# First dense layer of a graph network by groups of four destination tiles, with its sums kept turned

## The reference

```python
x = layernorm(x + attention_block(x, src, dst, etype))
h = x
for W_r, W_sl, W_el in [(W_r1, W_sl1, W_el1), (W_r2, W_sl2, W_el2)]:
    msg = (rel_embed[etype] + h[src]) @ W_r
    agg = segment_sum(msg, dst)
    self_msg = where(in_degree == 0, h @ W_el, h @ W_sl)
    h = rrelu(agg * deg ** -0.5 + self_msg)          # rrelu: slope 11/48 below 0
x = layernorm(x + h)
```

## Time and profile before

| | us |
|---|---|
| median of 3 runs | 2772.72 (2772.16 to 2774.16) |
| profiled execution | 2772.09 |
| its span in the trace | 2770.1 |
| POOL busy | 1590.8 (57%) |
| PE busy | 2148.2 (78%) |
| DVE busy | 2044.5 (74%) |
| ACT busy | 1222.7 (44%) |
| mean granted TensorE clock | 0.906 |

### The profile page before, as it was taken

One profiled execution on the slowest core, in us unless ns is written; L12 is line 12 of the kernel. 1 busy time (PEld: TensorE's weight loads), 2 busy tenths in 40 slices (PEclk: granted clock), 3 DMA queues, 4 the chain that ended last, 5 costly groups with the idle time before them and its releaser, 6 DMA issues.

```text
span 2770.1 us, 45483 instructions
## 1 busy us (share of the span) xinstructions
PE 2148.2 (78%) x16208; PEld 1803.9 (65%) x16208; DVE 2044.5 (74%) x4582; ACT 1222.7 (44%) x3215; POOL 1590.8 (57%) x1672
## 2 busy tenths in 40 slices
PE   1467666677677677787787788788787999999998
PEld 0355555566566566576676677667666876888887
DVE  6889998888888888898888888888887456333333
ACT  1265566555455555555555555555654323000000
POOL 6767777777777777777777777777774000000000
PEclk9888888888888888888889988999898999999999
DMA  8535554454554554554555555555444344666664
GB/s 222 164 117 166 174 172 141 149 176 146 157 181 145 157 182 150 154 184 152 166 176 157 169 175 164 172 169 174 154 153 153 108 157 135 215 209 212 215 211 158
DMA packets 184632, 463.50 MB, mean 167 GB/s; under 512 B 86336, under 2 KB 113784, under 8 KB 164577
## 3 DMA queue, kind: packets, MB, share of 16 engines
q1 hardware_dynamic: 116050, 339.10, 36.3%
q0 software_dynamic: 53600, 114.17, 15.8%
q10 hardware_dynamic: 14752, 7.26, 1.0%
HBM read 362.54 MB, written 97.84 MB: 166 GB/s over the span
## 4 chain that ended last, share of the span: by engine, by line
POOL 52%; PE 24%; issue 18%; DVE 4%; DMA 2%; ACT 0%; POOLq 0%; ACTq 0%; SPq 0%; DVEq 0%
POOL arena L568 52%; PE pair L960 19%; PE bank L884 1%; DVE arena L1124 1%; PE bank L845 1%; PE pair L933 1%; DMA wlp<-n_L_gnn_loop_weight_dram 1%; PE pair L963 1%; DMA group_starts<-endv 0%; DMA arena<-in_x_dram,srcw 0%; DVE arena L1101 0%; PE pair L814 0%; PE pair L791 0%; DVE arena L1071 0%; DVE arena L1072 0%
## 5 line engine op out<-in xcount | busy, mean ns | idle before, releaser
L568 POOL DMA_INDIRECT arena<-rows,srcw x1617 | 1540.4, 953 | 510.1 <-issue 492.2
L1124 DVE TENSOR_TENSOR arena<-bank,idx 128x2000 bf16<-128x2000 bf16 (+3 forms) x700 | 560.5, 853 | 22.4 <-PE pair L814 19.0
L960 PE MATMUL pair<-arena 125*125 125x384 bf16 x3285 | 551.4, 326 | 1.6 <-DVE arena L1325 1.6
L814 PE MATMUL pair<-arena 128*128 128x250 bf16 x2500 | 344.5, 285 | 262.2 <-DVE arena L1124 208.7
L590 ACT ACTIVATE arena<-pair 99x264 f32<-99x264 f32 (+2 forms) x410 | 278.8, 712 | 582.6 <-PE pair L814 448.9
L960 PEld LDWEIGHTS pair<-arena 125*125 125x125 bf16 x3285 | 447.4, 136 | 103.3 <-issue 8.4
L684 ACT ACTIVATE arena<-arena,wexp 128x128 f32<-128x128 bf16 x1650 | 487.4, 387 | 1.6
L884 PE MATMUL bank<-arena 128*125 128x130 f32 x3300 | 486.9, 319 | 0.0
L884 PEld LDWEIGHTS bank<-arena 128*125 128x125 f32 x3300 | 476.4, 230 | 3.9
L814 PEld LDWEIGHTS pair<-arena 128*128 128x128 bf16 x2500 | 237.8, 102 | 339.7 <-DVE arena L1124 271.5
L1101 DVE TENSOR_TENSOR arena<-arena,bank 128x4224 bf16<-128x4224 int16 x150 | 344.2, 2350 | 1.7
(11 more groups left out here) (250 smaller groups left out, 2311.5 us busy)
## 6 DMA issues: line engine op xcount, KB each, us to landing
arena<-counts SPq DMA_DIRECT2D x106, 812.5 KB, 4.4
counts<-arena SPq DMA_DIRECT2D x50, 1562.5 KB
arena<-dst SPq DMA_DIRECT2D x50, 1056.0 KB
arena<-etype SPq DMA_DIRECT2D x50, 1056.0 KB
arena<-rows,srcw POOLq DMA_INDIRECT x1617
arena<-counts SPq DMA_DIRECT2D x14, 281.2 KB, 2.7
edge_terms<-arena SPq DMA_DIRECT2D x200, 12.4 KB
xt<-in_x_dram SPq DMA_DIRECT2D x50, 62.5 KB
```

What stands on the lines that cost most here:

```text
L568: pool.indirect_dma_start(out=rows[:, q, c, :], out_offset=None, in_=rows0, in_offset=bass.IndirectOffsetOnAxis(ap=srcw[:, q, c:c + 1], ax ...
L814: r = pe.matmul(group_of(n, gi), ohl[:, sl, gi * GC + c, :], ohm[:, sl, gi * GC + c, :], start=(c == 0), stop=(c == GC - 1))
L960: r = pe.matmul(o, ring[0:TN, m % RD, h - h0, :], hs[k][0:TN, h, :], start=(h == first), stop=(h == last - 1))
L1124: return v.tensor_tensor(hot_.rearrange("p c (j t) -> p c j t", t=2), iotap[:, 0:w].rearrange("p (j t) -> p j t", t=2)[:, None, :, :].broa ...
```

## The change

The first layer's products are turned round: each 128-column part of `hs0` is a weight, and the counts of four destination tiles (500 columns) move. A **unit** is one source tile (or one half of the types) for a group of four destination tiles, and is three products of 500 columns into one bank, so that the three parts and all units add up there. The tiles make 13 groups (the last has two tiles) of 52 units. The sum stands turned (features on partitions), without the factor `norm`, in `acc`. That factor is put into layer 2's weights side instead (`scale=norm` in `node_a`), and the layer's own term is divided by it (`rstd`) and turned once (`own_turned`).

`row` and `early` go. In their place each tile t from 6 on has up to two **stretches** (t,0) and (t,1) of at most 12 units, all from counts loaded back in **chunks** of at most 4 units (512 KB, rows of 1000 B) into two buffers `held`. There are 80 stretches with 528 units in 154 chunks; 148 units are left behind the main loop, 40 of them for tiles 44 to 47 and 52 half-wide ones for tiles 48 and 49. 24 tiles have a third chunk in stretch (t,0): 9, 13, 17, 21, 22, 25, 26, 29, 30, 33, 34, 35, 37, 38, 39 and 41 to 49 (of 2, 3 and 1 units in tiles 9, 22 and 44, else of 4). The first chunk of (t,0) runs ahead of the sums (L884 before), the second and third behind the edge terms. Stretch (t,1) has up to 4 units until tile 30, 5 or 6 in tiles 31 to 40, 7 to 9 from tile 41 on.

The last tile's batches, which stood ahead of its `weights`, now stand behind them as in all tiles. `hot` shrinks to 26 slots, and some small tiles move into the arena.

```diff
 def sp_fast(sp):                      # the loop over t
+                load_held(t, 0, 1)
                 if t + 2 < NT:
                     load_wide(t + 2, f2)
-                if t in EARLY:
-                    load_early(t)
+                load_held(t, 0, 2)
                 if t + 1 < NT:
                     reshape_terms(t + 1)
                 else:
                     for m in range(RD):
                         load_piece(m)
+                load_held(t, 1, 0)
+                load_held(t, 1, 1)
                 if t < NT - 1:
                     store_x1(t)
+                load_held(t, 1, 2)
+                load_held(t + 1, 0, 0)
                 store_counts(t)
...
+            def load_held(t, k, i):
+                if (t, k, i) not in HELD_AT:
+                    return
+                n = HELD_AT[t, k, i]
+                key, g, u0, u1 = HELD[n]
+                if n >= 2:
+                    sp.wait_ge(s("held_done"), n - 1)
+                sp.wait_ge(s("at_stored"), 32 * GT * (g + 1))
+                sp.dma_start(held[:, n % 2, 0:GT * (u1 - u0) * TN].rearrange("p (t f) -> p t f", t=GT),
+                             counts[GT * g:GT * g + GT, :, u0 * TN:u1 * TN].rearrange("t p f -> p t f")).then_inc(s("held%d" % (n % 2)), 16)
...
 def pe_fast(pe):
+            def unit(o, moving, u, start, stop):
+                for j in range(3):
+                    js = slice(j * D, (j + 1) * D)
+                    if u < 2:
+                        n_ = (P, R2)[u]
+                        w = relW[0:n_, 0, u, js]
+                    else:
+                        n_ = TN
+                        w = hs0[0:TN, u - 2, js]
+                    r = pe.matmul(o, w, moving[0:n_], start=start and j == 0, stop=stop and j == 2)
+                return r
...
+            def stretch(t, k, i):
+                if (t, k, i) not in HELD_AT:
+                    return
...
+                if i == 0 and m >= 1:
+                    pe.wait_ge(s("st_read"), m)
+                if u1 > 2:
+                    pe.wait_ge(s("hs_ready"), u1 - 2)
+                pe.wait_ge(s("held%d" % (n % 2)), 16 * (n // 2 + 1))
...
             for t in range(NT):
...
+                stretch(t, 0, 0)
                 if t >= 1:
                     pe.wait_ge(s("fin"), t)
                 pe.wait_ge(s("wm"), NWM * t + 1)
...
                 if t + 1 < NT:
                     terms(t + 1)
-                if 1 <= t < NT - 1:
-                    row(t - 1)
+                stretch(t, 0, 1)
+                stretch(t, 0, 2)
...
+                    stretch(t, 1, 0)
+                    for j in range(4, BT):
                         batch(t, j)
-                    x1_in(t)
-                    batch(t, BT - 1)
-                    x1_node(t)
-                    if t in EARLY:
-                        early(t)
+                x1_in(t)
+                stretch(t, 1, 1)
+                x1_node(t)
+                stretch(t, 1, 2)
...
             for m in range(LOWER):                      # behind the main loop
+                k, g, u0, u1 = PIECES[m]
...
+                for u in range(u0, u1):
+                    if u == HS - 1 and g == 0:
+                        pe.wait_ge(s("hs_ready"), NT)
+                    r = unit(o, part[:, :, u - u0, :], u, u == DONE_U[g], u == HS - 1)
+                r.then_inc(s("piece_done"), 1)
...
+                if u1 == HS and g >= 1:
+                    for t in tiles_of(g - 1):
+                        node_m(t)
 def dve_fast(v, link):
             def weights(t):
+                if t >= 1:
+                    stretch_sum(t - 1, 1)
...
+            def stretch_sum(t, k):
+                v.wait_ge(s("held_done"), HELD_TO[t, k])
+                v.wait_ge(s("ev"), seq("node", GT * g + GT - 1) + 1)
+                a = acc[:, GT * g:GT * g + GT, 0:TN]
+                v.tensor_tensor(a, per_tile(bank[6][:, 0:GT * TN], GT), a, ALU.add).then_inc(s("st_read"), 1)
...
                     for j in range(2):
                         batch(t, j)
-                    prepare_edges(t + 1)
+                    if more:
+                        prepare_edges(t + 1)
+                    stretch_sum(t, 0)
                     batch(t, 2)
...
-                    batch(t, 4)
-                    row_sum(t - 1)
-                    for j in range(5, BT):
+                    for j in range(4, BT):
                         batch(t, j)
```

More of the change, by code:

```diff
@@ L75, with tiles_of @@
 L0_LINKS = 37
[L76 to L89, removed]
+GT = 4
+NGR = -(-NT // GT)
+HOTS = 26
+NU = 4
+SLEN = 3 * NU
+STRETCH, DONE_U = {}, [0] * NGR
+for t_ in range(6, NT):
+    for k_ in range(2):
+        best = None
+        for g_ in range(NGR - 1):
+            n_ = min(SLEN, t_ + 1 + k_ - DONE_U[g_])
+            if GT * g_ + GT + 1 <= t_ and n_ >= 2 and STRETCH.get((t_, 0), (NGR,))[0] != g_ and (best is None or n_ > best[0]):
+                best = (n_, g_)
+        if best is not None:
+            n_, g_ = best
+            STRETCH[t_, k_] = (g_, DONE_U[g_], DONE_U[g_] + n_)
+            DONE_U[g_] += n_
+STRETCHES = list(STRETCH)
+HELD, HELD_AT, HELD_TO = [], {}, {}
+for key_ in STRETCHES:
+    g_, u_, e_ = STRETCH[key_]
+    for i_ in range(-(-(e_ - u_) // NU)):
+        HELD_AT[key_ + (i_,)] = len(HELD)
+        HELD.append((key_, g_, u_ + i_ * NU, min(u_ + i_ * NU + NU, e_)))
+    HELD_TO[key_] = len(HELD)
+def tiles_of(g):
+    return range(GT * g, min(GT * g + GT, NT))
+PIECES, GROUP_TO = [], []
+for g_ in range(NGR):
+    each_ = RD_WORDS // (TN * len(tiles_of(g_)))
+    for u_ in range(DONE_U[g_], HS, each_):
+        PIECES.append((0, g_, u_, min(u_ + each_, HS)))
+    GROUP_TO.append(len(PIECES))
 LOWER = len(PIECES)
@@ L119 @@
             SEQ["turned", t_ + 1] = len(SEQ)
-    if t_ in EARLY:
-        SEQ["early", t_] = len(SEQ)
+    SEQ["node", t_] = len(SEQ)
 class Chain:
@@ L202, in build @@
         toh = carve([P, C, R], BF16)
+        HOTB_AT = at_[0]
         here(TOH_AT)
-        hot = carve([P, C, P])
-        HOTB_AT = at_[0]
+        hot = carve([P, HOTS, TN])
+        assert at_[0] <= HOTB_AT
+        here(HOTB_AT)
         hotb = carve([P, C, P], BF16)
@@ L676, in act_fast @@
                     node_b(0, t - 1)
-                if t == NT - 1:
-                    for j in range(BT):
-                        batch(t, j)
+                    own_turned(t - 1)
                 act.wait_ge(s("z_ready"), t + 1)
@@ L864, in pe_fast @@
                     self_in(t + 1)
-                else:
-                    row(t - 1)
-                    for j in range(BT):
-                        batch(t, j)
                 pe.wait_ge(s("th_ready"), t + 1)
@@ L883, in pe_fast @@
                         pe.wait_ge(s("wm"), NWM * t + c // WMG + 1)
-                    r = pe.matmul(sums[0:TN, 0:D + 2], hot[:, c, 0:TN], rows[:, q, c, 0:D + 2], start=(c == 0), stop=(c == C - 1))
+                    r = pe.matmul(sums[0:TN, 0:D + 2], hot[:, c % HOTS, :], rows[:, q, c, 0:D + 2], start=(c == 0), stop=(c == C - 1))
                     if c in ACC_AT:
```

351 lines of the change are left out of this document (159 added, 192 removed).

## The result

The changed kernel takes **2892.99 us** (median of 4 runs, 2886.86 to 2897.46) against 2773.22 of the kernel before: ratio 1.043, 95% interval 1.0418 to 1.0442. It is 120 us slower. The forecast was 2820, 48 slower, and its range ended at 2872: the direction was right, the size was not. The profiled execution has a span of 2893.2 us.

What follows compares the result with a forecast made beforehand. It took POOL's gathers (41.3 us a tile) to bound the main loop and PE the tail; 2772.1 - 48 (tail and last tiles) + 96 (lag from late third chunks) = 2820 us, slower, range 2735 to 2872.

Steps and rivals of the forecast that it cites:

- Tail: Behind the main loop: 61 + 17 + 12 x 3.75 + about 4 = 127 us, 51 us shorter than before.
- Last tiles: Batches now behind the last tile's sums: 42.5 us for tile 48, 40 for tile 49, ending 5 us later.
- The sum without a lag: Whole kernel with the main loop at POOL's pace: 51 + 2 - 5 = 48 us gained on 2772.1.
- Third chunk late: Main loop, stretch (t,0): the chunk lands at +29.9 behind the lists, PE idle from +20.0; lag adds up to 96 us.
- Rival (a): Third chunk isn't late, being served beside the lists; lag under 10 us, 2724 to 2734 us, faster; chance 0.13.
- What is behind the lists comes after them: SP's queue in the main loop: lists are through at +26.7, then the chunk's 512 KB lands at +28 to +30.7.
- I take 3.2: PE's time for the third chunk's products after idling, between 2.5 us at full clock and 5.1 at half.
- 3 us given back in each tile between: Main-loop tiles without a late third chunk have 2 to 5 us of room; each recovers 3 us of any lag.
- the wait for the gathers that I took as room: Main loop, tile 47: DVE waits 3.70 us for the gathers, read as some 3 to 4 us a tile free for work.
- the end of this lag: Main loop's upper case: chunk at +31, half clock, node product in full, 3 us more a tile, lag 150.

Runs made afterwards that it cites:

- a7: Changed kernel with the third chunk's load ahead of the lists and DVE's sum of (t-1,1) later, behind `u`: 2726.4 us.
- d12: Changed kernel with only the third chunk's load moved ahead of the lists: 2728.3 us, 0.9827 to 0.9860 of the kernel before.
- d14: Changed kernel with the third chunk's load issued from ACT's own DMA queue, not SP's: 2895.7 us, 1.0416 to 1.0464 of the kernel before.
- c10: Changed kernel with 88 unused products keeping PE busy between second and third chunk: 2862.9 us, 1.0309 to 1.0344 of the kernel before.
- b9: Changed kernel without the main loop's stretches (their loads, products and sums left out): 2711.4 us, 0.9770 to 0.9802 of the kernel before.

## Why the prediction was wrong in size

By its own steps:

- **Tail, right.** First tail product at 2335.99, first product of the second layer 2461.68: 125.7 us, forecast 127. From `u`(49) to the end: 599.2 us, forecast 40 + 127 + 434 = 601. The two 500-column sums of a group take 0.68 us each, forecast 0.66.
- **Last tiles, nearly.** `u`(48) to the first tail product: 85.4 us, forecast 82.5.
- **The sum without a lag, right.** 2772.1 - 48 = 2724. The kernels without the wait took 2726.4 and 2728.3 (a7, d12), and a7's `u`(49) is at 2121.8, where 2078.5 + 42.5 = 2121.0 was forecast.
- **Third chunk late, right, with its time.** Forecast +29.9; PE gets it at +28.4 to +31.1, +29.8 on average, in the 13 tiles from 33 on, and at +30.7 to +31.8 in the nine before them, where the edge terms end 1.7 us later too (+19.3). The idle time is 8.4 to 10.8 us, 9.5 on average, forecast 9.9. In tile 45 the chunk's packets move from +26.1 to +29.0. Rival (a) is out.
- **Its reason, half right.** "What is behind the lists comes after them" holds, but it isn't only the queue's order: with a queue of its own the chunk comes no earlier (d14).
- **"I take 3.2", wrong.** In nine of the 19 tiles with four units in the third chunk its products ran wholly at half the clock, as in tile 45: 5.16 us, 2.0 more. In the other ten they took 4.1 to 5.1. The prediction had 5.1 as its end and took the value between. DVE gets batch 2 at +36.0 on average, forecast +34.25, and the 22 tiles take 49.4 us: together 179.6 us over 41.25, where the steps have 134.6, that is 45 more, or 2.0 a tile. Of this c10 shows 30 as the clock's.
- **"3 us given back in each tile between", wrong.** The 17 tiles between tile 9 and 47 take 40.5 us and give back 13.2 us in all, where 38.6 were forecast: 25 more. The eleven up to tile 24 take 39.8 us on average and give back 1.5 each; the six from 27 on take 41.2 to 42.8 and give back nothing. b9 shows why for up to 1.9 us of each early one: the wait for the gathers that I took as room hid the wait for the node product. In the changed kernel `node_in` waits 2.0 us behind the third-chunk tiles up to 30, 0.6 from 33 to 35 and not at all from 37 on, so this doesn't explain the late ones, and no run separates what does.
- **The start.** At `u`(9) the changed kernel is already 7.1 us behind (475.46, before 468.40); no step had this. b9 is 3.5 behind there and has made it up by tile 11.

Together 7.1 + 179.6 - 13.2 - 1.4 (by which the kernel before is itself off 41.25 a tile) = 172.1, where 96 was forecast. The prediction gave 150 as the end of this lag, for a late chunk, half the clock and the node product in full; the first came in at its middle from tile 33 on, the second nearly in full, the third only in the tiles up to 30, and what was given back was not varied in that sum at all. That is why the range ended too early: 2820 + 76 = 2896.

## What to carry to other kernels

Before a load is issued beside a large one, look at the other one's bytes and at its packets: 512 KB in packets of 1 KB issued with 2.1 MB in packets of 8.4 KB landed at most 2 us behind those, from either queue. Put it ahead, or put the work that needs it behind work that doesn't; here the first is worth 165 us and the second 113. And the wait that ends last isn't room: it hides those that would come next, so take from it what the next one needs before you count on it.

## What the runs showed of the hardware that I had not expected

- Two DMA queues with work share the DMA engines by packets, not by bytes: 71 packets with 0.60 MB against 72 with 0.07 MB in 2 us, and 18 against 16 in half a microsecond (d14).
- The same program took 4487 us on a chip and later 2772 on the same one; in the longer runs PE, DVE and ACT are at rest for some 35 us a tile while the gathers go on. Only the kernel before, run beside each experiment, told the two apart.
